# Half of the attention's value product in high and low parts, with the moves, the projections and the layernorm placed anew

## The reference

```python
xn = (x - mean) / sqrt(var + 1e-5)
qkv = einsum('bsd,od->bso', xn, w_qkv)          # 16 heads of 128
q, k = rope(q), rope(k)
attn = softmax(einsum('bqhd,bkhd->bhqk', q, k) / sqrt(128))
out = einsum('bhqk,bkhd->bqhd', attn, v)         # the value product
attention = einsum('bso,do->bsd', out, w_out)
ffn = gelu(xn @ mxfp4(up) + up_bias) @ mxfp4(down) + down_bias
```

## Time and profile before

| | |
|---|---|
| median of 3 runs | 2506.6 us (2505.27 to 2508.3) |
| the profiled execution | 2508.02 us |
| its span, first to last instruction | 2506.2 us |
| granted TensorE clock, mean | 0.995 of full |
| busy share of the span | TensorE 98%, DVE 79%, ACT 57%, POOL 56% |
| DMA engines, mean busy share | 59.9%, 158 GB/s |

### The profile page before, as it was taken

How to read it: one execution, slowest core, us unless ns; L and a number is a source line. 1 busy time by engine, 2 the same in 40 slices (tenths; PEclk the granted TensorE clock), 3 DMA queues, 4 the chain that set the end, 5 groups by cost and what they waited for, 6 DMA issues and landing times. The chain is left out here.

```text
span 2506.2 us, 41398 instructions
## 1 busy us (share of the span) xinstructions
PE 2457.5 (98%) x12656; PEld 2139.8 (85%) x12656; DVE 1982.2 (79%) x3204; ACT 1437.6 (57%) x2648; POOL 1392.9 (56%) x1115
## 2 busy tenths in 40 slices
PE   6999999999999999999999999999999999999899
PEld 4888888888888888888888888888888888888688
DVE  6877878787887878788787878878787887878576
ACT  5656666565656566565656556655555566565233
POOL 6567656665655555565556555655555565555031
PEclk9999999999999999999999999999999999999999
DMA  4665666656665555656665655656575565655842
GB/s 135 167 168 151 173 159 161 172 157 189 179 163 147 151 153 153 157 146 188 173 164 143 160 150 151 159 146 185 152 183 146 151 159 152 158 140 144 231 141 68
DMA packets 267289, 396.28 MB, mean 158 GB/s; under 512 B 38496, under 2 KB 120800, under 8 KB 267104
## 3 DMA queue, kind: packets, MB, share of 16 engines
q1 hardware_dynamic: 267232, 395.67, 59.9%
HBM read 91.43 MB, written 35.65 MB: 51 GB/s over the span
## 5 line engine op out<-in xcount | busy, mean ns | idle before, releaser
L1020 PE MATMUL o_ps<-keys_first,v_rows 128*128 128x256 f32 x4096 | 930.9, 381 | 10.4 <-DMA keys_first<-turned_blocks 10.4
L1020 PEld LDWEIGHTS o_ps<-keys_first,v_rows 128*128 128x128 f32 x4096 | 767.7, 191 | 110.4 <-DMA keys_first<-turned_blocks 11.6
L1020 PE MATMUL s_ps<-seq_parts 128*128 128x512 f32 x3072 | 834.3, 409 | 12.7 <-ACT probs L689 8.0
L792 DVE TENSOR_REDUCE neg_max<-s_ps 128x1 f32<-128x1024 f32 x512 | 611.3, 1203 | 160.3 <-PE s_ps L1020 160.1
L689 ACT ACTIVATE probs<-s_ps,neg_max 128x1024 f32<-128x1024 f32 x512 | 568.7, 1111 | 247.9 <-DVE neg_max L792 241.7
L1020 PEld LDWEIGHTS s_ps<-seq_parts 128*128 128x128 f32 x3072 | 577.9, 189 | 133.6 <-ACT probs L689 12.1
L804 DVE STREAM_TRANSPOSE turned_blocks<-probs 128x512 f32<-128x512 f32 x1024 | 662.9, 685 | 32.2 <-ACT probs L689 10.3
L558 POOL TENSOR_TENSOR rope_a<-rope_a,cos 128x512 f32<-128x512 f32 x250 | 324.6, 1298 | 633.1 <-ACT rope_b L673 633.1
L563 POOL TENSOR_TENSOR seq_parts<-rope_a,seq_parts 128x512 fp32r<-128x512 f32 x250 | 320.5, 1282 | 288.4 <-ACT seq_parts L680 288.4
L1020 PE MATMUL slot_ps<-seq_parts,w_parts 128*128 128x512 f32 x1506 | 386.9, 392 | 4.8 <-DMA seq_parts<-xnt_parts 4.8
L680 ACT ACTIVATE seq_parts<-rope_a 128x512 fp32r<-128x512 f32 x250 | 157.6, 630 | 387.9 <-POOL rope_a L561 386.4
(11 more groups left out here) (111 smaller groups left out, 1733.6 us busy)
## 6 DMA issues: line engine op xcount, KB each, us to landing
keys_first<-turned_blocks SPq DMA_DIRECT2D x2048, 128.0 KB, 2.7
w_parts<-w_qkv_parts SPq DMA_DIRECT2D x72, 512.0 KB, 4.3
seq_parts<-xnt_parts SPq DMA_DIRECT2D x14, 1024.0 KB, 8.3
w_qkv_parts<-w_parts SPq DMA_DIRECT2D x24, 512.0 KB, 3.7
wo_parts<-w_out_parts SPq DMA_DIRECT2D x48, 256.0 KB, 3.1
w_raw<-in_w_qkv SPq DMA_DIRECT2D x24, 256.0 KB, 4.3
y<-in_x SPq DMA_DIRECT2D x16, 256.0 KB, 3.3
ln_x<-in_x SPq DMA_DIRECT2D x16, 256.0 KB, 3.4
```

Source lines behind the costliest of these rows:

```text
L792: nc.vector.tensor_reduce(neg_max[:, k2 % 16:k2 % 16 + 1], s_ps[k2 % 2][:, :], AXX, ALU.max, negate=True).then_inc(max_ready, 1)
L1020: ins = nc.tensor.matmul(out, w, m, start=(n == 0), stop=(n == len(terms) - 1))
```

## The change

1. **The value product.** Key tiles 0 to 3 (`SPLIT = 4`) are computed in high and low parts: `v_hi`, `v_lo` and `p_hi` (ACT, one 128x1024 copy a chunk, `probs_high`), and the low part of the probabilities, which is written over them in `keys_first` (`probs_low`: key tiles 0 and 1 always on POOL; tiles 2 and 3 on DVE in steps 0, 4, 5, 7 of a pair, on POOL in steps 1, 2, 3, 6). Each of the four tiles is three float32r matmuls; tiles 4 to 7 stay float32. `v_lo` is a DVE subtraction from PSUM, twice a pair.
2. **The moves.** One `turn` is one transposing instruction over 1024 keys, with a contiguous read. Query tile 0 of chunk k+1 is turned at the end of step k, tile 1 at the start of step k+1. Each tile is moved by itself, 4 DMAs with runs of 1 KB, 128 of them in each; before, 8 DMAs with 64 runs of 2 KB. The bytes are the same.
3. **Keys permuted.** As `turn` no longer interleaves, the keys of K are stored in the permuted order: the high and low parts of keys are written through `by_remainder`, which reads every fourth element.
4. **Projections.** The table `GROUPS` moves one group from step 3 to step 2 and changes the order of v and qk1 groups; POOL's rotary work is cut in a sum and a low part that stand in different places of its queue.
5. **Layernorm.** In the rounds, `mean` (two instructions with an accumulator) and `normalise` (four) run on ACT in place of DVE. `quantise` is cut into 13 parts over ten steps in place of 8 parts over seven.

```diff
-        v_rows = sb("v_rows", [P, 2, BT, 2 * HEAD])
+        v_rows = sb("v_rows", [P, 2, BT - SPLIT, 2 * HEAD])
+        v_hi = sb("v_hi", [P, 2, SPLIT, 2 * HEAD], F32R)
...
-        turned_blocks = sb("turned_blocks", [P, 2, QUADS, BT, 2, QUAD])
-        keys_first = sb("keys_first", [P, 2, QUADS, BT, 2 * QUAD])
+        turned_blocks = sb("turned_blocks", [P, 2, 2, QUADS, BT, QUAD])
+        keys_first = sb("keys_first", [P, 2, 2 * QUADS, BT, QUAD], F32R)
...
+        FRONT, BACK = slice(0, 2), slice(2, SPLIT)
+        BACK_BY_DVE, BACK_BY_POOL = (0, 4, 5, 7), (1, 2, 3, 6)
...
-        MX_PARTS = {0: (0,), 5: (1,), 6: (2,), 7: (3,), 8: (4, 5), 9: (6,), 11: (7,)}
+        MX_PARTS = {0: (2,), 2: (3,), 3: (4,), 6: (5,), 7: (6, 7), 8: (8, 9), 10: (10,), 11: (11,), 12: (12,), 15: (0, 1)}
...
+            def move_tile(c, k, t):
+
+                slot = k % 2
+                sp.wait_ge(blocks_turned, c * 2 + t + 1)
+                if t == 0 and c >= 2:
                     sp.wait_ge(o_ready, c - 1)
                 for a in range(QUADS):
...
+                    sp.dma_start(keys_first[:, slot, t * QUADS + a].rearrange("p j q -> p (j q)").bitcast(F32),
+                                 turned_blocks[a * QUAD:(a + 1) * QUAD, slot, t].rearrange("p b j q -> p b (j q)")
+                                 ).then_inc(keys_moved[k % 4], 16)
...
+        def by_remainder(a):
+
+            return a.rearrange("p (j k b) -> p j b k", k=QUAD, b=QUADS)
...
+            def probs_low(c, k):
+
+                slot = k % 2
+                pool.wait_ge(p_hi_ready, c + 1)
+                low = keys_first[:, slot, :, FRONT, :]
+                nc.gpsimd.tensor_tensor(low, low.bitcast(F32), p_hi[:, slot, :, FRONT, :].bitcast(F32),
+                                        ALU.subtract).then_inc(p_lo_front, 1)
+                if k % 8 in BACK_BY_POOL:
+                    low = keys_first[:, slot, :, BACK, :]
...
+            def probs_high(i, k):
+
+                act.wait_ge(keys_moved[k % 4], chunk_moves(i, k))
+                nc.scalar.activation(p_hi[:, k % 2], keys_first[:, k % 2, :, 0:SPLIT, :].bitcast(F32),
+                                     ACT.Copy).then_inc(p_hi_ready, 1)
...
+                nc.vector.transpose(turned_blocks[:, k % 2, n].rearrange("p b j q -> p j b q"),
+                                    probs[:, (2 * k + n) % 4, :].rearrange("p (j b q) -> p j b q", b=QUADS, q=QUAD)
+                                    ).then_inc(blocks_turned, 1)
...
-                chain(o_ps[:, 0:CHUNK],
-                      [(v_rows[:, parity, kt, cols], keys_first[:, slot, :, kt, :]) for kt in range(BT)], o_ready)
+                for kt in range(SPLIT, BT - 2):
+                    unsplit(kt, kt == SPLIT)
+                pe.wait_ge(p_hi_ready, c + 1)
+                for kt in range(SPLIT):
+                    nc.tensor.matmul(out, v_hi[:, parity, kt, cols], p_hi[:, slot, :, kt, :], start=False, stop=False)
+                    nc.tensor.matmul(out, v_lo[:, parity, kt, cols], p_hi[:, slot, :, kt, :], start=False, stop=False)
...
+                for kt in range(BT - 2, BT):
+                    unsplit(kt, False)
+                pe.wait_ge(p_lo_front, c + 1)
...
+                for kt in range(SPLIT):
+                    last = nc.tensor.matmul(out, v_hi[:, parity, kt, cols], keys_first[:, slot, :, kt, :],
+                                            start=False, stop=(kt == SPLIT - 1))
+                last.then_inc(o_ready, 1)
```

More of the change, by code:

```diff
@@ L479, in batch @@
                                      d["mx"][:, MX_COLS - MX_STEP:]).then_inc(mx_w_loaded[1], 16)
+                    if not (last and n == SEQ_CHUNKS - 1):
+                        move_tile(b * SEQ_CHUNKS + n + 1, n + 1, 0)
+            move_tile(0, 0, 0)
             batch(0, True, False)
@@ L539, in rotate @@
             eng.wait_ge(own, before * 4 + 2)
-            engine.tensor_tensor(hi, a, b, ALU.add).then_inc(own, 1)
+            engine.tensor_tensor(hi, a_in, b_in, ALU.add).then_inc(own, 1)
             eng.wait_ge(own, before * 4 + 3)
@@ L602, in step @@
                 p = i * 2 + k // 8
+                more_pairs = not (last and k >= 8)
                 more = splitting and not (isinstance(p, int) and p + 1 >= PAIRS_PER_SEQ)
@@ L938, in _ @@
             row_max(1, 1)
+            for (place, part, n), bank in zip(FIRST_GROUPS, FIRST_BANKS):
+                if part == "v" and n in V_SPLIT:
+                    v_low(0, 0, n, bank)
+            turn(0, 0, 0, True)
             def step(i, k, first, last):
@@ L945, in step @@
                 if not tail:
-                    turn(i, k, 0, first)
+                    turn(i, k, 1, first)
                 if has_out:
                     low_out(c - 2, k % 2)
-                if not tail:
-                    turn(i, k, 1, first)
+                g = None if tail or (first and k == 0) else group_at(k - 1, 1, last)
+                if g and g[1] == "v" and g[2] in V_SPLIT:
+                    v_low(i * 2 + g[3], g[3] % 2, g[2], slot_ps[:, 1])
                 if (k - 1, 1) == LN_SLOT:
@@ L960, in step @@
                     row_max(t + 3, 2 * k + 3)
+                if (k - 1) % 8 in BACK_BY_DVE and not (first and k == 0) and not (last and k == 17):
+                    probs_low(c - 1, k - 1)
+                g = None if tail else group_at(k, 0, last)
+                if g and g[1] == "v" and g[2] in V_SPLIT:
+                    v_low(i * 2 + g[3], g[3] % 2, g[2], slot_ps[:, 0])
                 if has_out:
@@ L963, in step @@
                     add_out(c - 2, (k - 2) % 16, (i // 4) if k >= 2 else ((i - 1) // 4))
-                if k == 0:
-                    dve.wait_ge(ln_loaded, (i + 1) * 16)
-                    mean(i + 2, ln_x, LN_COLS)
-                if k == 3:
+                if not tail and not (last and k == 15):
+                    turn(i, k + 1, 0, first)
+                if k == 4:
                     newton(i + 2, LN_COLS)
-                if k == 4:
-                    normalise(i + 2, ln_x, ln_xn, LN_COLS)
+                if first and k == 0:
+                    quantise(i, 0)
+                    quantise(i, 1)
                 for part in MX_PARTS.get(k, ()):
-                    quantise(i, part)
+                    if k < 15:
+                        quantise(i, part)
+                    elif not last:
+                        quantise(i + 1, part)
             steps(dve, step)
```

259 lines of the change are left out of this document (189 added, 70 removed).

## The result

| | before | changed |
|---|---|---|
| runs, median (lowest to highest), us | 2506.4 (2505.3 to 2508.3) | 2601.6 (2596.5 to 2602.9) |
| ratio | 1 | 1.0375, 95% interval 1.0357 to 1.0393 |
| profiled execution: time, span | 2508.0, 2506.2 | 2596.5, 2594.6 |

The forecast was 2455. The change costs 95 us instead of giving 51.

What follows compares the result with a forecast made beforehand. It took TensorE's own queue as the bound: 2508.0 - 74 + 12 + 9 + 1 = 2456, and 2455 us as the median of runs, 1.4 below the profiled one; range 2430 to 2490, with about 0.79 inside.

Steps and rivals of the forecast that it cites:

- The value product: TensorE's value product: twelve float32r matmuls at 0.12 us replace four float32 ones at 0.432 per chunk, 74 us less.
- (c): Value product: float32r matmuls on short runs cost more than 0.12 us; at 0.01 more each, 2486 us; chance 0.06.
- (d): Value product: float32r streams like a float32 record, 0.216 us, 0.86 more a chunk, 2728 us; chance 0.02.
- The loads: Work per pair of 70.0 us: POOL 57 us (62 in the first eight pairs), ACT 53, DVE 60 to 64.
- Rival (a): Moves cost by packet, so the chain through ACT outruns its slack: 2506 us, 2480 with half; chance 0.18.
- chain through ACT: From the moves through ACT's copy to o_lo, 9.0 to 10.6 us against 10.8 at the tightest; slack 0.2 to 1.8.
- No engine passes TensorE, but the cover is thin: Every other engine's load per pair stays below TensorE's 70.0 us, DVE nearest at 86 to 92%.
- That four parts on POOL read every fourth element I count at nothing too: POOL's strided reads cost no time, since 12 us of slack a pair covers them.
- Rival (b): POOL becomes the bound, its instructions slowed beside DVE: 1.64 us each is slower than before, 1.70 gives 2588; chance 0.07.
- The costs of 9 and 12 us: 9 us for moves colliding with loads of x between sequences, 12 us for the first eight pairs; both guesses.
- the 22 of costs: All costs added in the sum: 12 us first pairs, 9 us between sequences, 1 us ramp.

Runs made afterwards that it cites:

- e1_low_first: The changed kernel with POOL making the low part of chunk 1's probabilities ahead of the low part of queries qk1,3 in the third step: 2543.4 us.
- e7_after_shifted: The changed kernel with 216 more already-met waits ahead of TensorE's loop, the loop itself unaltered: 2565 us, ratio 1.0243.
- e8_low_shifted: The changed kernel with 216 already-met waits ahead of TensorE's loop and chunk 1's low probabilities ahead of the queries' low part on POOL; expected 2502 to 2512, measured time not given.

## Why the prediction was wrong

**The value product: right.** The product from its first record to the next scores takes 3.18 us, 3.46 before:

```profile
1013.13 1.03 PE L1258 MATMUL o_ps<-keys_first,v_rows 128*128 128x256 f32 x4
...
1016.31 1.53 PE L1185 MATMUL s_ps<-seq_parts 128*128 128x512 f32 x6
```

Records of a float32r product lie 0.12 apart, in runs of 32 elements as well (L1265 and L1266 from 1141.44 to 1141.81 above; only the first, 0.03 behind the record of a float32 product, is followed at 0.30, and the 3.18 us have that in them). The 74 us are there, and rivals (c) and (d) fall.
**The loads: right as means.** Each engine is within 2 us a pair of what I gave it, and the moves cost by the byte: 131072 packets more, half as many again, and nearly the same share of the queues, 59.7% for 59.9%. Rival (a) had the transfers wrong. Its chain through ACT does not hold TensorE in the steps either: the waits for `o_lo` behind ACT's wait for the move come to about 8 us, nearly all in the last steps, where the kernel before waited some 9 us for the same moves.

**The step that failed** is "No engine passes TensorE, but the cover is thin", and its twin "That four parts on POOL read every fourth element I count at nothing too: 12 us of slack a pair covers them". Slack of a pair is no slack of step 2. I walked one chain through its queue, that of `probs_high` through ACT, and not the other, that of `probs_low` through POOL, where the queries stand ahead of it and wait for ACT twice. Walked by the rows it was there to be had: POOL's three operations for their sum (3.9 us), ACT's high part 0.6, low part 1.3, then two of 1.3, behind ACT's copies of the group late in step 1. The strided reads add 0.28 us for each low part of keys (below), but the order costs the 58 us. Rival (b) had the sign, and for a wrong reason: POOL's operations take 1.30 us in the mean (465.68 us over 357), not 1.64, and it is never the bound.

**The term that was missing** is TensorE's own program: 37 us for where its loop lies. Nothing in the trace of before shows it (18 packets), and no term of the sum had a place for it. Nor had one a place for the clock: the changed kernel's 18 stretches at half clock lose it 36 us, the kernel before loses 14, e1_low_first 28 and e7_after_shifted 24, so a part of both gains is the clock's.

**The costs of 9 and 12 us** for loads of x and for the first pairs: the 9 did not come. TensorE's waits at the borders of sequences are `PE slot_ps L1185 <- DMA seq_parts<-xnt_parts: 5.8, 3, 2.0`, 4.8 us before. TensorE idles 14.1 us of 200 to 400 against 8.4 for each 200 later, and 38 in 60 to 600 against 23 at the later rate: the 12 of the first pairs roughly.

Together: 2602 = 2432 (the kernel before less 74) + 58 (POOL's order) + 37 (the place of the loop) - 11 (their sum is that much over what both give, within the noise) + 86 that stay: about 23 by POOL's back parts, some 15 to 20 at v_ready that only move on when ACT's order is changed, about 6 by the clock at half in e8_low_shifted, the rest spread over steps 2 and 3 and the ramp, and not taken apart further. The forecast missed by 147 us. POOL's order and the loop's place are 84 of them; the other 63 or so are the 86 less the 22 of costs that the sum had.

## What to carry to other kernels

Before an engine is given more work "in its slack", walk its queue in the one or two steps where what it makes is due soonest, with all that stands ahead of it and what that waits for; a mean load of 78% says nothing there. Splitting half as much gave half the gain in full, where the whole split lost it all. And read the instruction queue's packets in the page: when a loop that stayed begins to be fetched in each round, try moving it in the program before shortening it.

## What the runs showed of the hardware

- A loop of TensorE of 1667 or 1748 instructions is fetched once or in every round depending on where it lies in the program. The fetch makes TensorE idle 0.4 to 4.3 us at the branch and costs 23 to 37 us in 15 rounds.
- Behind some of TensorE's stalls the granted clock is half, 1.2 for 2.4 GHz (six score products in 2.92 us, not 1.73), so a stall can cost more than its length. The changed kernel has 18 such stretches, 72 us together, twelve of them in the steps behind the wait at L1277, idle for 0.9 to 1.9 us; the kernel before has 5, all before 70 us or after 2340 us.
- Reading every fourth element costs POOL 1.55 us, not 1.27, and ACT 1.15, not 0.62 (keys here; queries in the rows of 1133.12 above and 1132.41):

```profile
1128.40 1.55 POOL L597 TENSOR_TENSOR seq_parts<-rope_a,seq_parts 128x512 fp32r<-128x512 f32 x1
```

```profile
1125.59 1.15 ACT L770 ACTIVATE seq_parts<-rope_a 128x512 fp32r<-128x512 f32 x1
...
1132.41 0.62 ACT L770 ACTIVATE seq_parts<-rope_a 128x512 fp32r<-128x512 f32 x1
```
